# A four-stage network on one core: x loaded in pieces, a shorter FFN prelude, x parked inside the FFN loop, Mamba's constant rows made once

## The chip, the cores and the metric

The kernel runs on one core of a Trainium2 chip. The core has TensorE (PE; its weight loads are listed as PEld), VectorE (DVE), ScalarE (ACT), GpSimd (POOL) and SyncE (SP), which here only issues DMAs and handles semaphores. The metric is the device time of one execution in microseconds (us).

## The reference

The input x has 4,096 rows of 256 values. Four stages follow each other, and each adds a layer norm of its result to x:

```
x = x + LN(attention(LN(x)))     16 heads, causal linear attention, features elu + 1
x = x + LN(ffn(LN(x)))           256 -> 1024 -> 256, exact gelu
x = x + LN(mamba(LN(x)))         two layers, 512 channels, 16 states, a scan over all rows
x = x + LN(moe(LN(x)))           8 experts, the best 2 of each row
```

Three details matter here. The FFN's weights get a low-rank addition made of sixteen of its own input rows (rows 1 to 16 of LN(x)): W1 gets scale times the outer products of four pairs of them, W2 the same of four other pairs. The Mamba layers read LN(x) as their stream and add to it in place, so the x from before must be kept until the end of the stage. And a Mamba layer's velocity v = 0.6 v + input is computed as matrix products with constant powers of 0.6.

## The kernel before

All of x lies in SBUF as `x_res`: 32 tiles of 128 rows, the residual stream of all stages. A chunk is 512 rows, four tiles; there are NCH = 8. Each stage is a phase, `net.run(phase)`. A phase first raises its counting semaphores by one on SP (`start`, L88), then a barrier, then the work of the five engines side by side, each with an instruction order written out by hand, and at its end another barrier and the clearing of all its semaphores on SP (L99). Nothing of a phase starts before this is through.

**Start** (`build`, L2186, L2187): one DMA brings the 4 MB of x, a second the identity, and SP waits for both. Only then attention starts. Its six weight DMAs are issued at L189 to L194, and VectorE, ScalarE and TensorE all wait for them (`loaded`) first. VectorE makes the statistics of chunk 0 (L119, L123), GpSimd the inverse root (L111, L113), VectorE normalises (L234), TensorE transposes (L386), ScalarE copies (L326). Four projections (L395) follow, each into the one bank HEAD: ScalarE makes exp (L330, L334), VectorE the feature (L240), and only then the next projection may start.

**FFN** (`ffn_phase`): five weight DMAs (L518 to L522). Tile 0 is normalised (L552), and sixteen DMAs bring rows 1 to 16 of it from their partitions to partition 0 (L526). TensorE makes the products of the pairs: 8 calls for W1 (L633) and 32 for W2 (L642); each call in f32 is two instructions in the trace. VectorE adds them (L560, L564). Then the loop. TensorE: `hidden(i)` (L661), transposes `head(i+1)` (L652), `result(i)` (L670). VectorE: `head(i+1)` (statistics L119, L123, normalisation L576), `tail(i)` (L583, statistics of z, L590, x + z at L595). GpSimd makes the inverse root for each.

**Streaming in** (`stream_in`, `normalise_all`, a phase of its own): SP stores all of x to DRAM as `parked` in one DMA (L1450). VectorE makes the statistics of all 32 tiles, GpSimd one inverse root, and VectorE, after `parked` has landed, normalises x in place (L1480).

**Mamba** (`mamba_phase`, twice): SP issues 18 loads (L757 to L765), of which the last six are constant rows: three copies of powers of 0.6 in `Mf` and in `Gf`. All engines wait for all 18. VectorE then writes the bf16 high and low parts of these rows into the rows from SUB on of M2, once for each of its 2 * NSUB = 8 places: casts at L989 and L990, subtractions at L997, and the like into Gc (L992, L993, L999). `const_done` counts the two steps. ScalarE waits for the first of them ahead of the floor (L1124), GpSimd and TensorE for the second. GpSimd's first root (L890, L892) and with it the first normalised chunk (L1139), the transposes (L1272), the in-projection (L1284) and all that follows come behind that wait. TensorE first zeroes two banks (L1263). M2 is first read by the velocity products (L1372).

**MoE** (`moe_phases`) reads `parked` back in its first phase.

## Time and profile before

The median of three timed runs is 4020.06 us (4019.51 to 4025.07). The profiled execution took 4023.78 us, of which the trace spans 4022.0.

| stretch, us | what runs | PE busy, us | DVE busy, us | granted PE clock |
|---|---|---|---|---|
| 0 to 17.8 | x loaded | 0 | 0.0 | idle |
| 17.8 to 58.5 | attention's first chunk | 18.5 | 9.7 | 0.92 |
| 58.5 to 446.5 | attention | 370.7 | 226.0 | 0.83 |
| 446.5 to 495.3 | FFN prelude | 22.7 | 11.2 | 0.50 |
| 495.3 to 733.5 | FFN loop | 230.8 | 69.1 | 0.99 |
| 733.5 to 770.3 | streaming in | 0 | 23.2 | idle |
| 770.3 to 858.7 | Mamba 0, prelude | 28.5 | 33.8 | 0.64 |
| 858.7 to 2036.7 | Mamba 0 | 1033.2 | 852.7 | 0.95 |
| 2036.7 to 2125.3 | Mamba 1, prelude | 28.3 | 33.9 | 0.64 |
| 2125.3 to 3258.0 | Mamba 1 | 1017.0 | 852.1 | 0.97 |
| 3258.0 to 4022.0 | MoE | 517.3 | 426.4 | 0.79 |

Over the whole span PE is busy 81%, DVE 63%, ACT 48% and POOL 52%. A stretch's time is what counts for the sum; busy shares tell which engine could set it. The clock is the mean that the throttle granted to TensorE, 1.0 being full speed; where PE is idle it means nothing.

### The profile page before, as it was taken

How to read it: one execution, taken by the hardware profiler on the slowest of the kernel's cores; microseconds unless marked ns; L12 is line 12 of the kernel's file. 1: busy time of each engine (PE TensorE's matmuls, PEld its weight loads, DVE VectorE, ACT ScalarE, POOL GpSimd, SP SyncE). 2: the span in 40 equal slices, each digit the busy share in tenths (PEclk: the TensorE clock that was granted, in tenths of full speed). 3: DMA queues.
4: the chain of work that ended last, by engine and by line, in shares of the span. 5: the costliest groups of instructions: out<-in, count | busy, mean ns of one | idle time of the engine just before them, and what ended most of it. 6: DMA issues, size and time to landing. Idle time of an engine off the chain costs nothing. (4 is left out here: it accounts for less than half of the span.)

```text
span 4022.0 us, 67053 instructions
## 1 busy us (share of the span) xinstructions
PE 3267.0 (81%) x20668; PEld 2263.8 (56%) x20669; DVE 2538.1 (63%) x3759; ACT 1942.4 (48%) x4180; POOL 2075.5 (52%) x1328
## 2 busy tenths in 40 slices
PE   5999699269888988989938999898998843899970
PEld 3777566145555555555515555555555533788860
DVE  2656323547777777777736777777777767554545
ACT  1222022057666666666526766767667633233320
POOL 0000000137677777777725777877778765222216
PEclk8888699689999999999969999999999965899995
DMA  1000000113223222232212232322323234111113
GB/s 55 1 0 0 23 0 0 62 39 84 55 58 80 53 66 71 56 74 63 60 36 63 56 83 55 79 59 62 75 55 83 57 123 138 51 47 47 47 45 110
DMA packets 151616, 228.30 MB, mean 57 GB/s; under 512 B 25250, under 2 KB 84034, under 8 KB 149700
## 3 DMA queue, kind: packets, MB, share of 16 engines
q1 hardware_dynamic: 143300, 202.30, 18.7%
q0 software_dynamic: 8064, 23.08, 2.0%
q8 instruction: 105, 1.72, 0.2%
q14 instruction: 147, 1.20, 0.1%
HBM read 119.99 MB, written 23.59 MB: 36 GB/s over the span
## 5 line engine op out<-in xcount | busy, mean ns | idle before, releaser
L943 POOL TENSOR_TENSOR m_hc<-m_h,m_Cb 128x1024 f32<-128x1024 f32 x512 | 1234.5, 2415 | 413.0 <-PE m_bank L1354 255.3
L1080 DVE TENSOR_TENSOR_SCAN m_h<-m_dA,m_vel 128x1024 f32<-128x1024 f32 x512 | 1169.1, 2283 | 93.0 <-ACT m_dA L1220 50.0
L1354 PE MATMUL m_bank<-m_hc,ident 128*128 128x512 f32 x2048 | 1055.1, 630 | 102.4 <-POOL m_hc L943 102.1
L1220 ACT ACTIVATE m_dA<-m_delta,m_rate 128x255 f32<-128x255 f32 x2048 | 874.1, 497 | 46.2 <-DVE m_h L1080 26.0
L1370 PE MATMUL m_vel<-m_M,m_U 128*128 128x128 bf16 x4096 | 542.9, 222 | 76.1 <-DVE m_h L1080 58.3
L1354 PEld LDWEIGHTS m_bank<-m_hc,ident 128*128 128x128 f32 x2048 | 362.1, 197 | 323.2 <-issue 222.5
L1372 PE MATMUL m_vel<-m_M,m_U 112*128 112x128 bf16 x4096 | 542.7, 222 | 0.0
L1370 PEld LDWEIGHTS m_vel<-m_M,m_U 128*128 128x128 bf16 x4096 | 403.0, 99 | 211.1 <-DVE m_h L1080 102.2
L1372 PEld LDWEIGHTS m_vel<-m_M,m_U 112*128 112x128 bf16 x4096 | 407.0, 99 | 82.1 <-issue 70.3
L1284 PE MATMUL m_bank<-m_pair,m_in 128*128 128x256 f32 x1024 | 280.1, 401 | 68.8 <-DVE m_cv L1020 63.1
L1069 DVE TENSOR_TENSOR m_vel<-m_vel,m_entry 128x4 f32<-128x4 f32 x512 | 82.5, 161 | 366.8 <-PE m_vel L1372 363.8
L1284 PEld LDWEIGHTS m_bank<-m_pair,m_in 128*128 128x128 f32 x1024 | 194.8, 198 | 189.2 <-DVE m_cv L1020 100.1
L2037 ACT ACTIVATE x_h<-x_bank,x_b 128x256 f32<-128x256 f32 x320 | 134.4, 471 | 283.9 <-PE x_bank L1983 267.7
L1943 POOL DMA_INDIRECT x_x_in<-xn_rows,r_from_row x80 | 91.1, 1138 | 347.9 <-PE x_bank L1967 299.7
L1983 PE MATMUL x_bank<-x_xhi,r_wlo 128*128 128x256 bf16 x640 | 175.5, 274 | 5.7 <-issue 5.0
L111 POOL TENSOR_SCALAR var_eps<-a_zmv 128x1 f32<-128x1 f32 x32 | 7.1, 223 | 328.0 <-DVE a_zmv L299 328.0
L1983 PE MATMUL x_bank<-x_xlo,r_whi 128*128 128x256 bf16 x640 | 175.2, 274 | 0.0
L1983 PE MATMUL x_bank<-x_xhi,r_whi 128*128 128x256 bf16 x640 | 175.2, 274 | 0.0
L1996 PE MATMUL x_bank<-r_whi,x_hlo 128*128 x640 | 174.5, 273 | 0.0
L1996 PE MATMUL x_bank<-r_whi,x_hhi 128*128 x640 | 174.4, 273 | 0.0
L1996 PE MATMUL x_bank<-r_wlo,x_hhi 128*128 x640 | 174.4, 273 | 0.0
L933 POOL TENSOR_TENSOR m_u<-m_u,m_zs 128x1024 f32<-128x1024 f32 x34 | 80.0, 2352 | 172.2 <-DVE m_u L1055 172.2
(281 smaller groups left out, 5570.5 us busy)
## 6 DMA issues: line engine op xcount, KB each, us to landing
m_Cb<-m_c_rows SPq DMA_DIRECT2D x256, 256.0 KB, 3.2
m_M<-m_Mhi SPq DMA_DIRECT2D x128, 256.0 KB, 4.3
m_M<-m_Mlo SPq DMA_DIRECT2D x64, 256.0 KB, 3.9
m_U<-m_Uhi SPq DMA_DIRECT2D x128, 128.0 KB, 3.2
y_rows<-x_y SPq DMA_DIRECT2D x40, 256.0 KB, 2.1
m_U<-m_Ulo SPq DMA_DIRECT2D x64, 128.0 KB, 3.3
g_stage<-in_e_w SPq DMA_DIRECT2D x8, 1024.0 KB, 5.5
o_stage<-in_e_w SPq DMA_DIRECT2D x16, 512.0 KB, 4.2
```

The source lines that it names most:

```text
L943: nc.gpsimd.tensor_tensor(hc[:, g].rearrange("p m a t -> p m (a t)"), h[:, p % 2, 2 * g:2 * g + 2].rearrange("p m a t -> p m (a t)"), Cb[: ...
L1069: nc.vector.tensor_tensor(heads, heads, entry[:, p, 2 * g:2 * g + 2, :], ALU.add).then_inc(s["fix_done"], 1)
L1080: nc.vector.tensor_tensor_scan(flat(h), flat(dA), VB[:, 2 * g * 512:2 * (g + 1) * 512], 0.0, ALU.mult, ALU.add).then_inc(s["scan_done"], 1)
L1220: nc.scalar.activation(dA[:, p % 2, m, a, 1:CM], delta[:, par, m, 1:CM], ACT.Exp, scale=rate[:, m, NG * p + a:NG * p + a + 1]).then_inc(s[ ...
L1284: last = nc.tensor.matmul((H0, H1)[g % 2][:, m % 2 * CM:(m % 2 + 1) * CM], w_in[:, k, m * P:(m + 1) * P], xT[:, k, :], start=(k == 0), sto ...
L1354: last = nc.tensor.matmul(Y[g][:], net.ident[:], hc[:, g, :, a, :], start=(p == 0 and a == 0), stop=(p == NPAIR - 1 and a == NG - 1))
L1370: nc.tensor.matmul(to, U1[:, par, j, m * P:(m + 1) * P], M1[:, par, j, NG * p:NG * p + NG, :], start=True, stop=False)
L1372: last = nc.tensor.matmul(to, U2[:, par, j, m * P:(m + 1) * P], M2[:, par, j, NG * p:NG * p + NG, :], start=False, stop=True)
L1943: nc.gpsimd.indirect_dma_start(x_in[:, par, t, :], None, xn_rows, bass.IndirectOffsetOnAxis(from_row[:, at:at + 1], 0)).then_inc(s[f"x_in{ ...
L1983: last = nc.tensor.matmul(out, w_part[:, bass.ts(e * WB + kk * KH + m, P)], x_part[:, par, kk, :], start=(kk == 0 and n == 0), stop=(kk == ...
L1996: last = nc.tensor.matmul(YB[par][:, t * D:(t + 1) * D], h_part[:, par, m, t * P:(t + 1) * P], w_part[:, bass.ts(e * (WB // 2) + KD * KH / ...
L2037: last = nc.scalar.activation(h[:, g % 2, m % 2, :], HB[g][:, m % 2 * SLOT:(m % 2 + 1) * SLOT], ACT.Relu, bias=b1[:, bass.ts(e[par] * KH + ...
```

## The change

1. x is loaded by chunks. SP issues chunk 0 and the identity and waits for neither. The other seven follow in attention's block, behind its six weight DMAs. Each has a semaphore `x_in[c]`, for which VectorE waits ahead of a chunk's first statistics; TensorE waits for the identity. Behind them SP issues the FFN's five weight DMAs, into tiles that now live through both phases.
2. In attention's opening, ScalarE, TensorE and VectorE wait for the weights later. The four first projections go to the four banks S[g] without a wait between them, and the statistics of chunk 1 stand between the third and the fourth feature.
3. The FFN's sixteen token DMAs become two: a store of the sixteen rows to DRAM and, after a wait, a load of all onto partition 0. The products for W2 are 8 calls of 256 columns for 32 of 64, in another order of columns.
4. `stream_in` is gone. In the FFN's `tail(i)` VectorE also makes the statistics of the new x, SP stores each chunk to `parked` when its sum is done, GpSimd makes a third root per chunk, and `stream(i)` normalises the chunk in place once both are through. In the loop `stream(i-1)` stands ahead of `head(i+1)`.
5. In Mamba the six constant loads come first, with a semaphore of their own. VectorE makes the high and low rows for place 0 alone, and seven DMAs copy them to the other places of M2. TensorE waits for these ahead of the first velocity. ScalarE's wait for `const_done` is gone.

The core of the diff (semaphore declarations are left out):

```diff
 # build and attention
-                sp.dma_start(net.x, dram["x"].rearrange("(n p) d -> p n d", p=P)).then_inc(stored, 16)
-                sp.dma_start(net.ident[:], dram["ident"]).then_inc(stored, 16)
-                sp.wait_ge(stored, 32)
+                sp.dma_start(net.x[:, 0:TPC, :], net.x_rows[:, 0:TPC, :]).then_inc(net.x_in[0], 16)
+                sp.dma_start(net.ident[:], dram["ident"]).then_inc(net.ident_in, 16)
...
+                for c in range(1, NCH):
+                    tiles = slice(c * TPC, (c + 1) * TPC)
+                    sp.dma_start(net.x[:, tiles, :], net.x_rows[:, tiles, :]).then_inc(net.x_in[c], 16)
+                net.ffn.load(sp, dram)
...
                 for g in range(4):
-                    feature(0, 0, g)
+                    dve.wait_ge(qk_exp, 1 + g + 1)
+                    nc.vector.scalar_tensor_tensor(phi[:, 0, g, :], S[g][:], 0.0, exps[:, g % 2, :],
+                                                   ALU.max, ALU.add).then_inc(phi_done, 1)
+                    if g == 2:
+                        stats(1)
+                masks(0, 0)
                 normal(1)
-                masks(0, 0)
...
+                pe.wait_ge(loaded, LOADS)
+                pe.wait_ge(xT_done, 1 + KD)
                 for g in range(4):
-                    project(0, 0, g)
+                    for k in range(KD):
+                        last = nc.tensor.matmul(S[g][:], wqkv[:, k, g * P:(g + 1) * P], xT[:, 0, k, :],
+                                                start=(k == 0), stop=(k == KD - 1))
+                    last.then_inc(qk_psum, 1)
 # FFN
-                for r in range(4 * RANK1):
-                    sp.dma_start(tok[:, r, :], xn[1 + r:2 + r, 0, :]).then_inc(tok_done, 16)
+                sp.dma_start(tok_rows, xn[1:1 + 4 * RANK1, 0, :]).then_inc(tok_kept, 16)
+                sp.wait_ge(tok_kept, 16)
+                sp.dma_start(tok[0:1].rearrange("p r d -> p (r d)"), tok_rows.rearrange("r d -> (r d)").unsqueeze(0)).then_inc(tok_done, 16)
+
+                for c in range(NCH):
+                    sp.wait_ge(x_done, 1 + c + 1)
+                    if c >= 1:
+                        sp.wait_ge(parked, 16 * c)
+                    tiles = slice(c * TPC, (c + 1) * TPC)
+                    sp.dma_start(net.parked[:, tiles, :], x[:, tiles, :]).then_inc(parked, 16)
+                sp.wait_ge(parked, 16 * NCH)
...
-                for m in range(KH):
-                    r, half = m // 2, m % 2
-                    for i in range(RANK1):
-                        col = (m % 2) * D + i * (D // 4)
-                        last = nc.tensor.matmul(B[4 + m // 2][:, col:col + D // 4],
-                                                tok[0:1, 2 * (RANK1 + i) + 1, half * P:(half + 1) * P],
-                                                tok[0:1, 2 * (RANK1 + i), r:D:4], start=True, stop=True)
+                for i in range(RANK1):
+                    for half in range(2):
+                        to = B[4 + i][:].rearrange("p (r a o) -> p a r o", a=2, o=D // 4)[:, half]
+                        of = tok[0:1, 2 * (RANK1 + i), :].rearrange("p (o r) -> p r o", r=4)
+                        last = nc.tensor.matmul(to, tok[0:1, 2 * (RANK1 + i) + 1, half * P:(half + 1) * P], of,
+                                                start=True, stop=True)
...
+                def stream(i):
+                    dve.wait_ge(n_rstd, 1 + i + 1)
+                    dve.wait_ge(parked, 16 * (i + 1))
+                    for j in range(TPC):
+                        last = nc.vector.tensor_scalar(x[:, i * TPC + j, :], x[:, i * TPC + j, :], mv2[:, j, 0:1],
+                                                       rstd2[:, j:j + 1], ALU.subtract, ALU.mult)
+                    last.then_inc(n_done, 1)
+                    dve.wait_ge(n_done, 1 + i + 1)
+                    dve.sem_inc(net.carrier, 1)
 
                 head(0)
-                with dve.Fori(0, NCH - 1) as i:
+                head(1)
+                tail(0)
+                with dve.Fori(1, NCH - 1) as i:
+                    stream(i - 1)
                     head(i + 1)
                     tail(i)
+                stream(NCH - 2)
                 tail(NCH - 1)
+                stream(NCH - 1)
 # Mamba
+                for part in range(3):
+                    at = SUB + part * NS
+                    sp.dma_start(Mf[at:at + NS, 0], dram["decay"][SUB:SUB + NS]).then_inc(s["const_in"], 16)
+                    sp.dma_start(Gf[at:at + NS, 0], dram["carry_on"]).then_inc(s["const_in"], 16)
...
+                sp.wait_ge(s["const_done"], 1 + 2)
+                for at in range(1, 2 * NSUB):
+                    sp.dma_start(M2[SUB:KV, at // NSUB, at % NSUB], M2[SUB:KV, 0, 0]).then_inc(s["const_moved"], 16)
...
-                    for j in range(NSUB):
-                        nc.vector.tensor_copy(M2[SUB:SUB + 2 * NS, par, j], Mf[SUB:SUB + 2 * NS, 0])
-                        nc.vector.tensor_copy(M2[SUB + 2 * NS:KV, par, j], Mf[SUB + 2 * NS:KV, 0])
+                dve.wait_ge(s["const_in"], CONSTS)
+                for rows in (slice(SUB, SUB + 2 * NS), slice(SUB + 2 * NS, KV)):
+                    nc.vector.tensor_copy(M2[rows, 0, 0], Mf[rows, 0])
+                    last = nc.vector.tensor_copy(Gc[rows], on[rows])
+                last.then_inc(s["const_done"], 1)
                 dve.wait_ge(s["const_done"], 1 + 1)
-                for par in range(2):
-                    for j in range(NSUB):
-                        nc.vector.tensor_tensor(M2[SUB + 2 * NS:KV, par, j], Mf[SUB + 2 * NS:KV, 0],
-                                                M2[SUB + 2 * NS:KV, par, j], ALU.subtract)
+                nc.vector.tensor_tensor(M2[SUB + 2 * NS:KV, 0, 0], Mf[SUB + 2 * NS:KV, 0],
+                                        M2[SUB + 2 * NS:KV, 0, 0], ALU.subtract)
...
-                act.wait_ge(s["const_done"], 1 + 1)
...
+                        pe.wait_ge(s["const_moved"], COPIES)
```

## Rows read from the trace of the kernel before

**Rows 1.** Windows: stretch, its us, busy us (instructions) by engine, PEclk, DMA share, GB/s.

```profile
58.50:446.50 388.00, 370.70 (x2339) 292.76 (x2338) 226.03 (x580) 86.33 (x180) 33.57 (x76) 0.83 0.00 1
```

**Rows 2.** Timeline of the start: start us, us, engine, line, what, [idle before <-releaser].

```profile
0.74 0.45 SPq L2186 DMA_DIRECT2D x_res<-in_x  x1
17.80 0.33 SPq L189 DMA_DIRECT2D wqkv<-in_wqkv  x1
18.28 0.51 DVE L222 MEMSET a_vt<- 128x544 f32 x1
23.88 1.40 DVE L119 BATCH_NORM_STATS2 a_st<-x_res 128x6 f32<-128x256 f32 x4 [5.09 <-DMA parity<-in_parity]
33.87 3.78 PE L395 MATMUL a_bank<-a_xT,wqkv 128*128 128x512 f32 x4 [0.67 <-ACT a_xT L326]
38.97 0.69 DVE L240 SCALAR_TENSOR_TENSOR a_phi<-a_bank,a_exps 128x512 f32<-128x512 f32 x1 [8.40 <-ACT a_exps L334]
56.12 2.07 PE L405 MATMUL a_bank<-wqkv,a_xT 128*128 128x256 f32 x4 [2.07 <-DVE a_phi L240]
```

**Rows 3.** Timeline of the FFN prelude.

```profile
452.57 0.41 DVE L552 TENSOR_SCALAR f_xn<-x_res,f_mv,f_rstd 128x256 f32<-128x256 f32 x1 [1.18 <-POOL f_rstd L113]
464.59 7.19 PE L633 MATMUL f_bank<-f_tok 1*128 1x256 f32 x16 [21.45 <-DMA f_tok<-f_xn]
471.58 13.75 PE L642 MATMUL f_bank<-f_tok 1*128 1x64 f32 x64
495.28 4.93 PE L661 MATMUL f_bank<-f_xT,f_w 128*128 128x512 f32 x6 [1.30 <-ACT f_xT L611]
```

**Rows 4.** Timeline of one turn of the FFN loop.

```profile
669.46 13.90 PE L661 MATMUL f_bank<-f_xT,f_w 128*128 128x512 f32 x32
676.98 1.41 DVE L119 BATCH_NORM_STATS2 f_st<-x_res 128x6 f32 x4 [0.62 <-DVE x_res L595]
680.45 1.38 DVE L576 TENSOR_SCALAR f_xn<-x_res,f_mv,f_rstd 128x256 f32 x4 [1.66 <-POOL f_rstd L113]
683.19 1.04 PE L652 MATMUL f_bank<-ident,f_xn 128*128 128x128 f32 x8
698.12 13.90 PE L661 MATMUL f_bank<-f_xT,f_w 128*128 128x512 f32 x32
```

**Rows 5.** Timeline at the ends of the FFN and of Mamba's first layer.

```profile
732.27 1.23 DVE L595 TENSOR_TENSOR x_res<-x_res,f_zn 128x1024 f32<-128x1024 f32 x1
770.32 0.34 SPq L757 DMA_DIRECT2D m_norm<-in_m_norm  x1
2027.33 0.69 DVE L1061 TENSOR_TENSOR x_res<-x_res,m_bank 128x512 f32<-128x512 f32 x1 [7.96 <-PE m_bank L1343]
2036.75 0.34 SPq L757 DMA_DIRECT2D m_norm<-in_m_norm  x1
```

**Rows 6.** Timeline of Mamba's first prelude.

```profile
780.79 0.26 ACT L1118 ACTIVATE m_rate<-m_rate 128x64 f32<-128x64 f32 x1 [9.18 <-DMA m_Gf<-in_carry_on]
793.59 0.20 ACT L1124 ACTIVATE m_floor<-m_floor 128x1 f32<-128x1 f32 x1 [12.26 <-DVE m_Gc L993]
795.76 0.40 ACT L1133 ACTIVATE m_pair<-x_res 128x256 f32<-128x256 f32 x1
803.19 0.19 POOL L890 TENSOR_SCALAR m_mean<-m_ssq 128x2 f32<-128x2 f32 x1 [29.07 <-DVE m_Gc L999]
806.53 0.70 PE L1272 MATMUL m_bank<-ident,m_pair 128*128 128x128 f32 x4
814.73 1.99 PE L1284 MATMUL m_bank<-m_pair,m_in 128*128 128x256 f32 x8 [2.85 <-DVE m_cv L1020]
```

**Rows 7.** DMA issues: out<-in, queue, count, KB of each, median us from issue to landing.

```profile
x_res<-in_x SPq DMA_DIRECT2D x1, 4096.0 KB, 13.9
g_residual<-parked SPq DMA_DIRECT2D x8, 512.0 KB, 4.6
out_x<-x_res SPq DMA_DIRECT2D x8, 512.0 KB, 3.1
m_c_rows<-m_small SPq DMA_DIRECT2D x32, 16.0 KB, 1.4
```

More of the change, by code:

```diff
@@ L65, in __init__ @@
         self.own_pool = ctx.enter_context(nc.semaphore("own_pool"))
+        self.x_rows = dram["x"].rearrange("(n p) d -> p n d", p=P)
+        self.x_in = [ctx.enter_context(nc.semaphore(f"x_in{c}")) for c in range(NCH)]
+        self.ident_in = ctx.enter_context(nc.semaphore("ident_in"))
     def sb(self, ctx, name, shape, dt=F32):
@@ L103, in _, with __init__, load @@
                         sp.sem_clear(used)
+class FfnWeights:
+    LOADS = 5 * 16
+    def __init__(self, net, ctx):
+        self.w1 = net.sb(ctx, "f_w1", [P, KD, HID])
+        self.w2 = net.sb(ctx, "f_w2", [P, KH, D])
+        self.b1 = net.sb(ctx, "f_b1", [P, KH])
+        self.b2 = net.sb(ctx, "f_b2", [P, D])
+        self.scale = net.sb(ctx, "f_scale", [P, 1])
+        self.loaded = ctx.enter_context(net.nc.semaphore("f_loaded"))
+    def load(self, sp, dram):
+        sp.dma_start(self.w1[:], dram["f_w1"]).then_inc(self.loaded, 16)
+        sp.dma_start(self.w2[:], dram["f_w2"]).then_inc(self.loaded, 16)
+        sp.dma_start(self.b1[:], dram["f_b1"]).then_inc(self.loaded, 16)
+        sp.dma_start(self.b2[:], dram["f_b2"].partition_broadcast(P)).then_inc(self.loaded, 16)
+        sp.dma_start(self.scale[:], dram["f_scale"].partition_broadcast(P)).then_inc(self.loaded, 16)
 def inverse_root(net, pool, out, variance):
@@ L2185, in _ @@
             def _(sp):
-                sp.dma_start(net.x, dram["x"].rearrange("(n p) d -> p n d", p=P)).then_inc(stored, 16)
-                sp.dma_start(net.ident[:], dram["ident"]).then_inc(stored, 16)
-                sp.wait_ge(stored, 32)
+                sp.dma_start(net.x[:, 0:TPC, :], net.x_rows[:, 0:TPC, :]).then_inc(net.x_in[0], 16)
+                sp.dma_start(net.ident[:], dram["ident"]).then_inc(net.ident_in, 16)
+        with ExitStack() as weights:
+            net.ffn = FfnWeights(net, weights)
+            net.run(attention_phase)
+            net.run(ffn_phase)
         for phase in phases:
-            if phase in (mamba_phases, moe_phases):
-                phase(net)
-            else:
-                net.run(phase)
+            phase(net)
 def layout(a):
```

143 lines of the change are left out of this document (51 added, 92 removed).

## The prediction, made before the changed kernel ran

> **What bounds the kernel now.** I read the busy times per stage first, in the table of windows. The two Mamba layers take 2,355 us, and inside their loops the work is shared by four engines; the change leaves these loops as they are. The places it touches are the seams between the stages, so the question at each seam is which wait ends last. I then read the timeline at each seam, and the DMA issues for transfer times.
>
> Five stretches matter. Until 17.8 us no engine computes: everything waits for x, one DMA. Then x's statistics wait 5.1 us more, until 23.88, for the last of six small loads that they don't use [rows 2]. After it the first four projections share one PSUM bank, so matmul, ScalarE and VectorE alternate until 56.12 [rows 2]. Attention's own loop then has PE nearly always busy, yet the mean granted clock is 0.83 [rows 1]. In the FFN prelude PE idles 21.45 us for sixteen small DMAs and then runs 80 instructions at the lower clock [rows 3]. The FFN loop is bound by PE: hidden, transposes and result follow each other without a gap, 28.66 us a chunk (669.46 to 698.12 [rows 4]). Between 733.5 and 770.3 PE is idle. In each Mamba prelude the constant rows, made eight times over on VectorE, release GpSimd, TensorE and ScalarE [rows 6].
>
> **The change, part by part.** All sums are made against the profiled execution, 4023.78 us by its own time (span 4022.0), which is 3.7 above the median 4020.06.
>
> *1. x in pieces.* SP now issues x's first 512 KB at 0.74 and the identity, waits for nothing, and is through at about 1.7. Starting a phase costs semaphore operations. Between the two Mamba layers 130 of them (66 cleared, 64 raised) take from 2028.02 to 2036.75, 8.73 us, or 0.067 each [rows 5]; attention raises 32, 2.1 us, so its block starts near 3.9. Two memsets take until 1.0 us after that [rows 2]. A 512 KB transfer lands 3.1 to 4.6 us after its issue [rows 7], so at 3.8 to 5.3. I take the statistics at 5.1, against 23.88: **-18.8**. The weights, first in the queue of the new block, land some 6.1 us after its start as before (23.88 - 17.80), at 10.0. They are needed by the first projection, 10.0 us after the statistics (33.87 - 23.88), at 15.1, so they are covered. The other seven pieces and the FFN's 2.1 MB are queued behind them; 4 MB took 13.9 us [rows 7], so all lie in SBUF long before VectorE reaches them.
>
> *2. Four banks for the first projections.* Before: 33.87 to 56.12, 22.25 us, in four rounds of about 5.8 (3.78 matmul, about 1.3 on ScalarE, 0.69 on VectorE [rows 2]). Now 16 matmul instructions of 512 columns run back to back. At the lower level one takes 0.86, at the higher 0.43 (32 in 13.90 [rows 4]). When the FFN starts the same way, 6 take 4.93 [rows 3] and all later ones are fast. So the groups end at about 3.8, 5.9, 7.6 and 9.3. Behind the last: ScalarE 1.3. But VectorE now makes the second chunk's statistics (1.8) between the third and the fourth feature: it starts them at 9.6, ends at 11.4, and the fourth feature ends at 12.2. Gain 22.25 - 12.2 = **-10**; with the clock low to the end, the last group ends at 14.0 and the gain is 6.2; without the interposed statistics it would be 11.
>
> *3. FFN prelude.* Weights come early: no gain by itself, as they had landed before the first product. Token rows: their source is ready at 452.98, and the first product waits until 464.59 [rows 3]. Now one 16 KB store and, after its wait, one 16 KB load. A 16 KB store lands in 1.4 [rows 7]. The load I bound between 1.4 and 4.6 and take at 2.0, nearer to the small one. The product starts near 456.6: -8.0. The second product has 16 instructions of 256 columns for 64 of 64. Such a one took 7.19/16 = 0.45, so 7.2 for 13.75: -6.6. Five more semaphores raised: +0.3. Together **-14.3**; with the load at 4.6 it would be -11.7.
>
> *4. The parking and the streaming in the FFN loop.* This adds a wait. In each loop turn VectorE now goes: stream(i-1), head(i+1), tail(i). stream(i-1) waits for GpSimd's root and for the parking DMA of the sum just made; head(i+1) is queued behind it, and PE's transposes wait for head(i+1). Let T be the start of hidden(i), 669.46 in the turn I read [rows 4]. x's sum is done at T+6.9 (676.98 less 0.62). From the start of statistics to the start of the normalisation that uses them takes 3.47 (676.98 to 680.45). So the streaming statistics, begun at T+7.1, allow the normalisation at T+10.6; the parking DMA lands at T+10.1 to T+11.6 (3.1 to 4.6). The normalisation takes 1.38, so head(i+1) starts at T+12.1 instead of T+7.5, and its own normalisation at T+15.6 instead of T+11.0. PE's transposes start at T+13.7 now and end at T+14.8 [rows 4]. In the changed kernel they wait for the first tile until about T+16.1 and for the fourth until T+17.0, and end at T+17.3. PE stalls 2.5 us a turn. head(0) and head(1) come ahead of tail(0), so six turns pay: **+15**. If the parking lands at 4.6, each pays 1 more: +21. What would hide this is slack of VectorE ahead of the transposes; there are 2.7 us of it (T+13.7 less T+11.0), and about 4.7 are added.
>
> *5. The tail and the dropped pass.* Before, the last sum ends at 733.50 [rows 5] and Mamba starts at 770.32: 36.8. Now the last chunk's statistics and root allow its normalisation after 0.2 + 3.5, the parking after 3.2 to 4.7; with 1.4 for it the block ends about 5.3 later. 27 semaphores are then cleared and 64 raised, 91 times 0.067 = 6.1, and some 0.3 of barriers. Mamba starts 11.8 after the sum: **-25**, or -24 with the later landing.
>
> *6. Mamba's constant rows.* VectorE's 24 large operations (16 casts, 8 subtractions) become 3, and 7 DMAs copy the result to the other places. The constants are loaded first, so VectorE ends before the 18 loads have landed, which they do 10.5 us after the block's start (780.79 - 770.32) [rows 6]. ScalarE's floor was released only at 793.59; now at 781.3, after the two small rate operations. From there to the end of the squares takes 2.6 (796.16 - 793.59). GpSimd takes them up near 784.2, against 803.19, where it was released by the constants. PE's zeroing products (3.75 us) moved ahead of the gap, no longer in the way. So **-19** for each of the two layers, -38. The largest load is issued 2.8 us later, which may cost up to 1.5 a layer; and the zeroing products no longer lead straight into the transposes, so that the next 16 products may run at the lower level, up to 3.7 more. Seven more issues on SP sit ahead of its first store, over 20 us before that is wanted; the copies themselves are first needed by the velocity products, over 60 us after the start. Both cost nothing; without that cover, about 4 us a layer.
>
> Sum: -18.8 - 10 - 14.3 + 15 - 25 - 38 = -91. From 4023.8 that gives 3932.7; from the median, 3929. I say 3930.
>
> **A rule that speaks against it.** In the preludes PE resumed after 2.85 us without work at full pace, 8 products of 256 columns in 1.99 [rows 6], the higher level (2.4 GHz). So my sum has the stall of 2.5 us in part 4 without a price in clock. The Trainium skill (TensorE: Matmul & The Clock Gate, "HAM oscillation — how this bites in real kernels") warns that idle waits between groups of matmuls let the clock fall again, each group then starting cold. By the row that rule costs nothing here; by the rule, taken for every stall, the time is the first rival's.
>
> **The rivals.**
> - *The clock falls at each stall.* For it: attention has a mean clock of 0.83 though PE is busy 370.7 of 388 us [rows 1]. Against: the 2.85 us gap. The FFN's first hidden ran 4.3 us at the lower level (495.28 to 499.6) [rows 3], which costs 2.15. Six times: +13, 3943. Chance 14%.
> - *No stall in the loop.* VectorE would have to find 2.5 us. Nothing in the rows gives them. 3930 - 15 = 3915. Chance 10%.
> - *The weights share the DMA engines with x's other pieces and the FFN's weights*, and land after 6.8 MB instead of first; at 4 MB in 13.9 us that is 24 us after 3.9. The first projection waits until 27.9 instead of 15.1: +13, 3943; +5 if only x's pieces interfere. Against it: one queue, weights first. 9%.
> - *Slower.* In the FFN loop the stall keeps PE at the lower level (1.2 GHz) for good. A chunk takes 57.3 instead of 28.66; eight chunks cost 229: 4159. It decides from 91/28.7 = 3.2 such chunks on. For it: attention's loop spends about a third of its time low. Against: its matmuls are short, and the FFN's, even with the stall, keep PE busy nine tenths of the time. 2%.
>
> **Numbers.** The forecast holds 65%. A measurement of this kernel tells about 0.2%, 8 us. Range 3910 to 3952: below, no stall and a short landing; above, the clock rival with a late parking. Only the last rival lies above 4020: faster 0.97, same 0.01, slower 0.02.
>
> **What would show it.** VectorE's first statistics near 5 us; the fourth first feature 12 us after the first projection; the first token product about 4 us after its row; in the FFN loop a PE gap of 2 to 3 us ahead of six of the transposes, released by VectorE, and turns of 31.2 us; Mamba's start 12 us after the last sum; GpSimd's first root 14 us after each Mamba start. A gain under 70 or over 115 would mean that a loop I called unchanged has moved.

## The result, and the profile after

Changed kernel: 3916.81 us, median of 4 runs (3912.37 to 3922.45); before, on the same chip, 4019.78 (4015.5 to 4025.07). Ratio 0.9744, 95% interval 0.9727 to 0.9761: faster by 103 us. The profiled execution took 3916.93, its span is 3915.0 (before 4022.0), so 107.0 us have to be found. The table has the landmarks of the two traces.

| landmark | before | after | difference so far | this step | forecast |
|---|---|---|---|---|---|
| first statistics | 23.88 | 5.13 | -18.75 | -18.75 | -18.8 |
| first projection | 33.87 | 13.77 | -20.10 | -1.35 | 0 |
| first tile's values | 56.12 | 25.66 | -30.46 | -10.36 | -10 |
| last sum of attention ends | 446.48 | 411.72 | -34.76 | -4.3 | 0 |
| first hidden product of the FFN | 495.28 | 446.78 | -48.50 | -13.7 | -14.3 |
| last sum of the FFN ends | 733.50 | 708.06 | -25.44 | **+23.1** | +15 |
| Mamba's first layer starts | 770.32 | 719.78 | -50.54 | -25.1 | -25 |
| GpSimd's first root there | 803.19 | 735.52 | -67.67 | -17.1 | -19 |
| Mamba's second layer starts | 2036.75 | 1927.32 | -109.43 | **-41.8** | 0 |
| GpSimd's first root there | 2070.04 | 1943.15 | -126.89 | -17.5 | -19 |
| MoE starts | 3259.04 | 3151.72 | -107.32 | **+19.6** | 0 |

The seams are where they were forecast. The two largest departures lie inside Mamba's loops, whose code is the same in both kernels.

The start after, answering [rows 2] (timeline: start us, us, engine, line, what, [idle before <-releaser]):

```profile
4.22 1.28 ACT L359 ACT_TABLE_LOAD   x1 [4.06 <-PEq L91]
5.13 1.34 DVE L142 BATCH_NORM_STATS2 a_st<-x_res 128x6 f32<-128x256 f32 x4
13.77 9.23 PE L514 MATMUL a_bank<-a_xT,wqkv 128*128 128x512 f32 x16 [0.77 <-ACT a_xT L359]
24.95 0.66 DVE L337 SCALAR_TENSOR_TENSOR a_phi<-a_bank,a_exps 128x512 f32<-128x512 f32 x1
25.66 1.13 PE L439 MATMUL a_bank<-wqkv,a_xT 128*128 128x256 f32 x4 [2.66 <-DVE a_phi L337]
```

The statistics no longer wait for a DMA: they stand right behind the memset. The 16 projections are one run of 9.23 us (forecast 9.3), and the fourth feature starts 11.2 after it began. The 1.35 us I had not counted: ScalarE's table load (1.28 us) now lies at 4.22, ahead of the data; before, it stood at 30.14, behind the first transposes and ahead of the copy which the first projection needs.

The FFN's prelude, answering [rows 3] (same columns):

```profile
418.19 0.41 DVE L605 TENSOR_SCALAR f_xn<-x_res,f_mv,f_rstd 128x256 f32<-128x256 f32 x1 [1.18 <-POOL f_rstd L136]
418.63 0.34 SPq L562 DMA_DIRECT2D tok_rows<-f_xn  x1
420.07 0.27 SPq L564 DMA_DIRECT2D f_tok<-tok_rows  x1
422.40 7.19 PE L710 MATMUL f_bank<-f_tok 1*128 1x256 f32 x16 [14.00 <-DMA f_tok<-tok_rows]
429.39 7.43 PE L719 MATMUL f_bank<-f_tok 1*128 1x256 f32 x16
446.78 2.07 PE L737 MATMUL f_bank<-f_xT,f_w 128*128 128x512 f32 x2 [1.31 <-ACT f_xT L688]
```

Store and load together take 3.8 us from the finished row to the first product, 0.2 more than forecast.

One turn of the FFN loop, answering [rows 4]:

```profile
641.05 13.90 PE L737 MATMUL f_bank<-f_xT,f_w 128*128 128x512 f32 x32
648.11 1.40 DVE L652 BATCH_NORM_STATS2 f_st<-x_res 128x6 f32 x4 [0.16 <-DVE x_res L648]
651.95 1.38 DVE L664 TENSOR_SCALAR x_res<-x_res,f_mv,f_rstd  x4 [1.91 <-POOL f_rstd L136]
653.68 1.41 DVE L142 BATCH_NORM_STATS2 f_st<-x_res 128x6 f32 x4 [0.35 <-DVE x_res L664]
657.16 1.38 DVE L629 TENSOR_SCALAR f_xn<-x_res,f_mv,f_rstd 128x256 f32 x4 [1.65 <-POOL f_rstd L136]
657.62 1.41 PE L728 MATMUL f_bank<-ident,f_xn 128*128 128x128 f32 x8 [2.68 <-DVE f_xn L629]
672.69 1.88 PE L737 MATMUL f_bank<-f_xT,f_w 128*128 128x512 f32 x4
```

The chain has the forecast order: the streaming statistics at T+7.1, the normalisation of x at T+10.9 (T = 641.05), released by GpSimd's root and not by the parking, then the next chunk's statistics at T+12.6, and PE waits 2.68 us for VectorE ahead of its transposes. The turn is 31.64. Of the six turns with a stall three are like this one and three are 33.2 to 33.3. Windows of one of each:

```profile
576.07:607.72 31.65, 28.97 (x105) 18.94 (x104) 12.42 (x41) 7.75 (x11) 3.79 (x6) 1.00 0.05 17
607.72:641.05 33.33, 30.66 (x106) 20.13 (x105) 12.41 (x41) 7.74 (x11) 3.79 (x6) 0.95 0.05 16
```

(Stretch, its us, busy us (instructions) of PE, PEld, DVE, ACT and POOL, PEclk, DMA share, GB/s.) In the longer turn the granted clock is at the lower level for 3.4 us, from 1.4 us after PE has resumed. (The first turn, 31.12, has no stall; PE starts it at the lower clock, as before.)

The seam to Mamba and Mamba's first prelude, answering [rows 5, 6]:

```profile
706.83 1.23 DVE L648 TENSOR_TENSOR x_res<-x_res,f_zn 128x1024 f32<-128x1024 f32 x1
719.78 0.34 SPq L834 DMA_DIRECT2D m_Mf<-in_decay  x1
731.90 0.26 ACT L1196 ACTIVATE m_rate<-m_rate 128x64 f32<-128x64 f32 x1 [10.83 <-DMA m_decay<-in_decay]
731.92 3.42 PE L1340 MATMUL m_bank<-m_hc,ident 128*128 128x512 f32 x4 [30.48 <-DMA m_decay<-in_decay]
735.52 0.19 POOL L970 TENSOR_SCALAR m_mean<-m_ssq 128x2 f32<-128x2 f32 x1 [11.95 <-ACT m_pair L1210]
739.17 6.63 PE L1361 MATMUL m_bank<-m_pair,m_in 128*128 128x256 f32 x16 [0.93 <-ACT m_pair L1221]
```

ScalarE and PE are now released by the loads, no longer by the constants. They land 12.1 us after the block's start, not 10.5: that is the 1.5 us a layer which the forecast allowed and did not count. The 16 products that follow run in part at the lower clock, 6.63 us for 3.72 before, as the forecast also allowed; it costs nothing here, since from GpSimd's first root to the first addition to x it is 85.4 us after and 85.2 before.

Mamba's loops. I measure a turn from one addition to x (L1139) to the next; windows: stretch, its us, busy us (instructions) of PE, PEld, DVE, ACT and POOL, PEclk, DMA share, GB/s. After, second layer, a short turn and a long one:

```profile
2313.95:2384.47 70.52, 65.11 (x408) 40.97 (x407) 54.00 (x58) 48.86 (x108) 54.31 (x30) 0.95 0.27 67
2384.47:2460.53 76.06, 66.97 (x408) 42.60 (x407) 54.32 (x58) 49.11 (x108) 54.31 (x30) 0.93 0.25 63
```

Same instructions, nearly the same busy time on VectorE, ScalarE and GpSimd, 1.9 us more on TensorE, and 5.6 us more in all. I call a turn long when it takes over 73 us. Every second turn is such a long one, but only in some layers: six in the first layer before and none in the second, none and five after. From first to last addition the two loops take 1138.9 + 1098.0 = 2236.9 us before and 1096.9 + 1117.0 = 2213.9 after. So the loops give -23.0 and all the rest -84.0.

### The profile page after: what moved, and what is told of

The parts are those of the page before. It is cut to its first block and busy times, and to the rows that moved or that the text cites. A ratio compares the mean times of both kernels' runs of the same rounds, so it can differ in the third digit from the quotient of the medians.

```text
span 3915.0 us, 67006 instructions
## 1 busy us (share of the span) xinstructions
PE 3257.2 (83%) x20620; PEld 2255.4 (58%) x20621; DVE 2504.7 (64%) x3717; ACT 1942.4 (50%) x4180; POOL 2077.8 (53%) x1340
## 5 line engine op out<-in xcount | busy, mean ns | idle before, releaser
L1448 PE MATMUL m_vel<-m_M,m_U 128*128 128x128 bf16 x4096 | 542.8, 222 | 89.0 <-DVE m_h L1158 65.1
L1448 PEld LDWEIGHTS m_vel<-m_M,m_U 128*128 128x128 bf16 x4096 | 402.8, 99 | 222.6 <-DVE m_h L1158 110.3
```

The costliest lines, as they stand in the source:

```text
L1448: nc.tensor.matmul(to, U1[:, par, j, m * P:(m + 1) * P], M1[:, par, j, NG * p:NG * p + NG, :], start=True, stop=False)
```

## The experiments

"Loops" is the sum of the two Mamba loops as just defined, from each run's profile; "rest" is the span less that. Each ratio is to the kernel before as timed on the same chip as the run (medians 4016.67 to 4022.40).

| kernel | median us | ratio to before, 95% interval | span | loops (turns over 73 us by layer) | rest |
|---|---|---|---|---|---|
| before | 4019.78 | | 4022.0 | 2236.9 (6, 0) | 1785.1 |
| changed | 3916.81 | 0.9744 (0.9727-0.9761) | 3915.0 | 2213.9 (0, 5) | 1701.1 |
| e1 head first | 3898.40 | 0.9697 (0.9675-0.972) | 3898.6 | 2216.0 (0, 5) | 1682.6 |
| e2 old constants | 3982.00 | 0.9912 (0.989-0.9934) | 3979.4 | 2244.9 (4, 6) | 1734.5 |
| e3 pass apart | 3940.42 | 0.9799 (0.978-0.9819) | 3943.5 | 2237.7 (4, 5) | 1705.8 |
| e4 shift | 3926.62 | 0.9767 (0.9746-0.9788) | 3925.0 | 2214.4 (0, 5) | 1710.6 |
| e5 changed again | 3916.68 | 0.9743 (0.9726-0.9759) | 3917.5 | 2211.7 (0, 5) | 1705.8 |
| e6 body of four | 3888.10 | 0.9674 (0.9657-0.969) | 3885.8 | 2205.7 (2, 2) | 1680.1 |
| e7 old token rows | 3900.35 | 0.9706 (0.969-0.9722) | 3897.6 | 2211.5 (0, 4) | 1686.1 |
| e8 one bank | 3908.77 | 0.9727 (0.9711-0.9743) | 3903.3 | 2211.7 (0, 3) | 1691.6 |
| e9 before, straight | 3970.27 | 0.9884 (0.9854-0.9914) | 3972.3 | 2190.3 (0, 0) | 1782.0 |
| e10 changed, straight | 3885.14 | 0.9673 (0.9652-0.9693) | 3883.7 | 2179.5 (0, 0) | 1704.2 |
| e11 head first, straight | 3862.10 | 0.9614 (0.9597-0.9632) | 3856.1 | 2181.0 (0, 0) | 1675.1 |
| e12 late weights | 3900.15 | 0.9706 (0.9688-0.9724) | 3897.9 | 2215.9 (0, 5) | 1682.0 |

**e1: the next head ahead of the stream.** Tests the stall of part 4.

```diff
 with dve.Fori(1, NCH - 1) as i:
-    stream(i - 1)
     head(i + 1)
+    stream(i - 1)
     tail(i)
```

> The changed kernel with one edit: in VectorE's FFN loop the next chunk's head stands ahead of stream(i-1), as before the change. Theory (the stall is a matter of queue order): the head's normalisation is back near T+13 from the start of a turn, PE's transposes wait for nothing, turns are 28.7 us instead of the 31.7 and 33.3 measured, the FFN's part (first hidden to last sum) falls from 261.3 to about 239, and the time from 3916.8 to about 3895. Rival (the third statistics and root simply overload VectorE and GpSimd in the loop): turns stay above 31 us and the time within 5 us of 3917.

One turn in e1 (timeline):

```profile
538.15 13.90 PE L737 MATMUL f_bank<-f_xT,f_w 128*128 128x512 f32 x32
547.54 1.41 DVE L142 BATCH_NORM_STATS2 f_st<-x_res 128x6 f32 x4 [0.41 <-issue]
551.01 1.38 DVE L629 TENSOR_SCALAR f_xn<-x_res,f_mv,f_rstd 128x256 f32 x4 [1.65 <-POOL f_rstd L136]
551.88 1.04 PE L728 MATMUL f_bank<-ident,f_xn 128*128 128x128 f32 x8
566.81 3.60 PE L737 MATMUL f_bank<-f_xT,f_w 128*128 128x512 f32 x8
```

The head comes at T+9.4 in place of T+12.6, the transposes wait for nothing, and the turn is 28.66 again. From the first hidden product to the last sum's end it is 238.8 us, against 261.3: 22.5 of the table's +23.1 were VectorE's order.

**e2: Mamba's constants as before**, all else changed. That part of the change taken back: VectorE makes the constants eight times over, and the others wait for them.

```diff
-for rows in (slice(SUB, SUB + 2 * NS), slice(SUB + 2 * NS, KV)):
-    nc.vector.tensor_copy(M2[rows, 0, 0], Mf[rows, 0])
+for par in range(2):
+    for j in range(NSUB):
+        nc.vector.tensor_copy(M2[SUB:SUB + 2 * NS, par, j], Mf[SUB:SUB + 2 * NS, 0])
+        nc.vector.tensor_copy(M2[SUB + 2 * NS:KV, par, j], Mf[SUB + 2 * NS:KV, 0])
...
```

> The changed kernel with Mamba's constant rows as before the change (loads last, 16 casts and 8 subtractions on VectorE, ScalarE's wait back). Theory (the preludes gave 17 us each and Mamba's loops are untouched): 3916.8 + 34 = 3951. Rival (the 23 us by which the two Mamba loops together became shorter in the trace come from where their turns fall against TensorE's clock, which every edit ahead of them shifts): the two loops' lengths change again, by 7 us for each turn with a second stretch at the lower clock, and the time lies anywhere between 3925 and 3990; the trace shows how many turns of over 74 us there are.

The rest grows by 33.4, the part's real worth (preludes -17.1 and -17.5 in the table). The loops grow by 31.0, with ten long turns for five (and three more of 72.4 to 72.9). A reading of the total alone would have called the constants worth 65 us.

**e3: the parking and normalisation as a pass of their own**, between FFN and Mamba, as before.

```diff
 with dve.Fori(1, NCH - 1) as i:
-    stream(i - 1)
     head(i + 1)
     tail(i)
...
+net.run(lambda n: stream_in(n, net.parked))
```

> The changed kernel with the parking and normalising of x as before, in a pass of its own after the FFN (its FFN loop is that of before too; some unused semaphores are still cleared, 0.4 us). Theory: the FFN's turns are back at 28.66 us, which gives back 23 us, and Mamba starts 37 us after the last sum instead of 11.7, which costs 25: 3916.8 + 2 = 3919, apart from what Mamba's loops do. Rival (the fused pass is worth its 25 us in full): 3942.

The rest grows by 4.7 only: the pass costs 25.5 more between the stages (Mamba starts 37.2 after the last sum, in the changed kernel 11.7), and the FFN loop, at 28.66 a turn again, gives 23.3 back (238.0 us for 261.3). As it was written, streaming into the FFN's tail was worth next to nothing. The other 24 us by which the span grows are the loops; by the total alone, 3940, the rival's 3942 would have been right.

**e4: a shift of 50 semaphore operations on SP ahead of Mamba**, nothing else.

> The changed kernel with 50 more semaphore operations on SP between the FFN and Mamba, nothing else: a shift of 3.3 us. If Mamba's loops don't depend on when they start: 3916.8 + 3.3 = 3920. If the number of turns with a second low stretch of the clock depends on it, the two loops (1126.4 and 1146.5 in the trace) change by several us, up to 20 either way.

The loops don't move (2214.4); the rest grows by 9.5, of which the 50 operations are 3.2 and attention 4.4. Mamba starts 7.5 us later in all, and the same turns are long.

**e5: the changed kernel once more.**

> The changed kernel once more, unchanged, on another profile. The question is Mamba's loops: in the profile of the changed kernel the first layer's loop had no long turn and the second's five (73 to 79 us in place of 70.5), in that of the kernel before six and none. Theory A: which turns are long belongs to the program (the address of its code, the order of its waits), and this run shows 0 and 5 again, loops of 1097 and 1117 us, 3915 to 3920 us as a whole. Theory B: it is drawn anew in each execution: another pattern than 0 and 5, and the time scatters with it, by up to 40 us for two layers with long turns against two without. If A holds, differences of the loops between kernels are repeatable but still no part of the edit.

The same pattern, (0, 5), and loops within 2.2 us. The long turns belong to the program. What does change between two executions of one program is attention: from the first tile's values to the start of its last sum 385.6 us in the first profile and 390.2 here; before took 389.9, and all fourteen profiles lie between 383.4 and 390.2. The -4.3 in the table can't be told from this scatter.

**e6: four chunks to a loop body.**

```diff
-with pe.Fori(1, NCM // 2 - 1) as c2:
-    slots(c2 * 2, 0, True, True)
-    slots(c2 * 2 + 1, 1, True, True)
+with pe.Fori(0, NCM // 4 - 1) as c4:
+    for n in range(4):
+        slots(c4 * 4 + 2 + n, n % 2, True, True)
```

(on all engines; VectorE and SP have their first two chunks ahead of the loop.)

> The changed kernel with the next turn's head ahead of the last one's stream in the FFN (as e1), and in Mamba the loop body written out for four chunks in place of two, so that each layer goes round its loop 3 times in place of 6 or 7 on every engine. The long turns of the Mamba loops were always every second one, those that hold the way back to the loop's start. Theory A: the way back costs it (fetching code again, engine by engine, until TensorE waits long enough for its clock to fall): then at most 2 to 3 turns of a layer are long, the loops together take 2194 + at most 20 us, against 2216 in e1, and the time falls by 5 to 15 us to 3883 to 3893. Rival B: the long turns follow the buffers' parity or the engines' order at even chunks: they stay at every second turn, 5 or more in a layer, and the time stays at 3898 or goes over it. Rival C: the longer code costs something of its own and all turns grow: over 3905.

Windows of e6, second layer:

```profile
2295.28:2365.35 70.07, 64.40 (x408) 40.17 (x407) 53.98 (x59) 48.85 (x108) 54.27 (x30) 0.98 0.27 68
2365.35:2439.80 74.45, 65.70 (x408) 42.15 (x407) 54.15 (x59) 49.07 (x108) 54.35 (x30) 0.95 0.25 65
```

In each layer two turns are long (over 73 us), from chunk 5 to 6 and from 9 to 10, exactly the two at which a body of four goes back; with bodies of two they were 3 to 4, 5 to 6, and so on to 11 to 12, and in some layers also 1 to 2, where only VectorE and SP, whose loops start with the first chunk, go back. They follow the way back, and not the parity of the buffers.

What happens there, in the changed kernel, around 2435 us (PE, then ScalarE):

```profile
2435.42 0.29 PE L1448 MATMUL m_vel<-m_M,m_U 128*128 128x128 bf16 x1 [2.84 <-issue]
2436.47 3.73 PE L1431 MATMUL m_bank<-m_hc,ident 128*128 128x512 f32 x4
2433.95 1.70 ACT L1297 ACTIVATE m_dA<-m_delta,m_rate 128x255 f32<-128x255 f32 x4 [1.84 <-issue]
```

The 16 small matmuls at the top of PE's body stop after six for 2.84 us, and "issue" says that the engine waited for nothing which the profile shows. ScalarE stops likewise. Then the clock is down: four products on m_hc take 3.73 us, where shortly after, at 2442.54, the same four take 1.93. So this long turn is a stop of TensorE of about 3 us plus what the clock costs after it.

That is not the account of all of them. ScalarE's stop is in every layer with a loop of two chunks, 1.6 to 2.6 us at each of its five ways back, also where no turn is long: the first line below is from the changed kernel's first layer. In the first layers of e2 and e3 it is VectorE that stops, for 3.2 to 3.6 us at each of its six ways back (second line, e2), and TensorE at most 1.0. In before's first layer, which has the longest turns, neither has such a stop by name (TensorE at most 0.8); there VectorE's scan waits 6.23 us, ended by ScalarE, and TensorE's in-projection 5.36 for VectorE (last two lines, before). Which stop is behind that wait the profile doesn't tell.

```profile
1222.28 1.70 ACT L1297 ACTIVATE m_dA<-m_delta,m_rate 128x255 f32<-128x255 f32 x4 [2.19 <-issue]
1244.08 2.29 DVE L1156 TENSOR_TENSOR_SCAN m_h<-m_dA,m_vel 128x1024 f32<-128x1024 f32 x1 [3.27 <-issue]
1304.21 2.29 DVE L1080 TENSOR_TENSOR_SCAN m_h<-m_dA,m_vel 128x1024 f32<-128x1024 f32 x1 [6.23 <-ACT m_dA L1220]
1309.14 2.07 PE L1284 MATMUL m_bank<-m_pair,m_in 128*128 128x256 f32 x4 [5.36 <-DVE m_cv L1020]
```

In e6's four long turns too it is VectorE that stops (3.3 to 3.6), and TensorE at most 0.9. And not every stop makes a turn long: in e7 and e8, of ten stops of TensorE of 2.4 us and more, three lie in turns of 71.3 to 72.3.

**e7: the token rows by 16 DMAs** (on e1).

```diff
-sp.dma_start(tok_rows, xn[1:1 + 4 * RANK1, 0, :]).then_inc(tok_kept, 16)
-sp.wait_ge(tok_kept, 16)
-sp.dma_start(tok[0:1]..., tok_rows...).then_inc(tok_done, 16)
+for r in range(4 * RANK1):
+    sp.dma_start(tok[:, r, :], xn[1 + r:2 + r, 0, :]).then_inc(tok_done, 16)
```

> As e1 (next turn's head first in the FFN), with the 16 token rows again fetched by 16 separate DMAs of one row each on SP, in place of one DMA to memory and one back; the FFN's weights still come early. My theory: of the 14.1 us that the FFN's prelude lost, the DMAs carry about 9 (the kernel before issued the last row some 12.9 us after the normalised row, the changed one has all 16 after 3.8) and the weights' early loading the rest; so the first hidden matmul comes 8 to 10 us later than in e1 (449.4), and the time is about 3907. Rival: the weights' wait was what ended last, and the rows cost nothing: 3898.

```profile
418.02 10.10 SPq L563 DMA_DIRECT2D f_tok<-f_xn  x16
429.32 7.19 PE L709 MATMUL f_bank<-f_tok 1*128 1x256 f32 x16 [21.53 <-DMA f_tok<-f_xn]
```

SP needs 10.10 us to issue them. From the start of attention's last sum to the first hidden product it is 42.99 us, in e1 35.38: the two DMAs are worth 7.6 (forecast 8.0). The median moves by only 2: attention was 3.2 us and the loops 4.5 us shorter in this profile.

**e8: the first projections through one bank** (on e1).

```diff
-for g in range(4):
-    for k in range(KD):
-        last = nc.tensor.matmul(S[g][:], ...)
-    last.then_inc(qk_psum, 1)
+for g in range(4):
+    project(0, 0, g)
```

> As e1 (next turn's head first in the FFN), with the first chunk's four projections again through one bank, so that each waits for the feature map of the one before it, as in the kernel before; x in pieces and all else kept. My theory: the values of the first tile start 10 us later (35.7 in place of 25.7 us from the start), all of it on the chain, and the time is about 3908. Rival: part of the 10 us is taken back in the attention loop, whose TensorE clock then comes up with other idle stretches before it: the last attention sum starts less than 5 us later than in e1 (413.99), 3898 to 3903.

The values start at 35.72, 10.1 later than in e1, and the last attention sum 8.6 later. Attention scatters by up to 4.6 us between two executions (e5), so the 8.6 alone could be more or less; but the median moves by 10.4 as well. The gain of part 2 reaches the end nearly whole, and the rival's 3898 to 3903 doesn't hold.

**e12: the FFN's weights late** (on e1): `net.ffn.load(sp, dram)` in the FFN's block.

> As e1 (next turn's head first in the FFN), with the FFN's weights loaded only at the FFN's start, ahead of the token rows on the same queue, as the kernel before did; the rows still go by two DMAs. Of the 14.1 us which the prelude lost, e7 put 7.6 on the rows (last attention sum to first hidden matmul 42.99 in e7, 35.38 in e1). Theory: the weights are the rest, since they stand ahead of the rows on SP and share the DMA engines with them: 4 to 7 us from the last attention sum to the first hidden matmul, and the time about 3904. Rival: the weights come while the stall on the rows lasts anyway, and the rest is clock: under 2 us, 3898 to 3900.

```profile
417.55 0.48 SPq L562 DMA_DIRECT2D tok_rows<-f_xn  x1
423.87 0.27 SPq L564 DMA_DIRECT2D f_tok<-tok_rows  x1
426.17 7.19 PE L710 MATMUL f_bank<-f_tok 1*128 1x256 f32 x16 [19.08 <-DMA f_tok<-tok_rows]
```

The store's wait ends 6.3 us after its issue, behind 2.1 MB of weights, where it took 1.4 in the changed kernel; from attention's last sum to the first hidden product 40.56, +5.2. Time: 3900, as attention was 3.7 shorter here. The two edits depend on each other: by SP's 16 issues, 10.10 us long, the weights are hidden, and beside one short store they are not. Of the table's -13.7 the products for W2 are 6.3 (7.43 us for 13.75). From the last sum to the first hidden product e7, with the old rows, early weights and new products, takes 42.99, and before less these 6.3 takes 42.9: early weights alone give nothing. e12, with new rows and late weights, takes 40.56: new rows alone give 2.4. Both together give 7.5.

**e9, e10, e11: no loop at all.** All 16 chunks of Mamba written out, in the kernel before, in the changed one, and in e1:

```diff
-with pe.Fori(1, NCM // 2 - 1) as c2:
-    slots(c2 * 2, 0, True, True)
-    slots(c2 * 2 + 1, 1, True, True)
+for c in range(2, NCM - 2):
+    slots(c, c % 2, True, True)
```

> The kernel before with Mamba's 16 chunks written out one after the other on every engine, no loop at all; the rest as before. In its profile the two loops took 2236.9 us (six long turns in the first layer), without long turns they would take about 2194. Theory A, that the way back to the loop's start is what makes a turn long: no long turn, the loops 2190 to 2200, the time about 3980. Rival B: straight code costs as much where it must be fetched: long turns stay or all turns grow, 4020 or more.

> The changed kernel, likewise with no loop in Mamba. Theory A: its loops fall from 2213.9 to about 2194, the time from 3917 to about 3897; against e9, with the loops' long turns out of both, the change is then worth what stands outside the loops, 84 us (my sum said 91). Rival B: 3917 or more; or the distance to e9 is the 103 us of the two medians, and then the loops had no part in it.

> The changed kernel with the next turn's head first in the FFN (as e1) and with no loop in Mamba: all that has been found in one kernel. Theory A: 3898.4 less the 22 us of long turns in e1's loops, 3876 to 3880, 8 to 12 below e6 with its four chunks to a body. Rival: the three turns back of e6 cost about what the longer code costs, and it ends at e6's 3888 or above.

One turn of e11's second layer (windows), and then the idle time of PE ahead of the velocity matmuls over seven turns, in e11 (L1444) and in the changed kernel (L1448; 2097 to 2605 us):

```profile
2136.66:2206.52 69.86, 62.79 (x408) 39.78 (x407) 54.10 (x59) 48.87 (x108) 54.27 (x30) 1.00 0.27 68
```

```profile
L1444 PE MATMUL m_vel<-m_M,m_U x896: 216/219/314, 2067.6 to 2553.4; 128*128 128x128 bf16 x180
its engine sat idle before it (us, times) until:
  DVE m_h L1156: 16.7, 7
  issue: 0.9, 2
```

```profile
L1448 PE MATMUL m_vel<-m_M,m_U x896: 219/219/314, 2099.2 to 2602.3; 128*128 128x128 bf16 x180
its engine sat idle before it (us, times) until:
  DVE m_h L1158: 15.5, 8
  issue: 9.1, 5
```

No turn is over 71.7 us, on no layer of the three kernels, and the unexplained stops of TensorE here fall from 9.1 to 0.9 us. The loops take 2190.3, 2179.5 and 2181.0. In e10 and e11 that is below the 2194 which I took as the floor, so both came in lower than expected (3885 for 3897, 3862 for 3876 to 3880): the short turns of a loop, at 70.5, cost more than the 70.0 of straight code. Straight code isn't all alike either: in e9's second layer five turns in a row take 71.7, and its loops are 10.8 longer than e10's. These five are the turns in which GpSimd's unexplained stops add up to most, 4.0 us; whether they are the cause no run shows. e11 is the best version: 3862.10 us, ratio 0.9614 (0.9597 to 0.9632), against 0.9744 for the change as given. And e9 against e10, both without a way back, leaves the change itself: spans -88.6, medians -85.1; outside the loops -77.8, where the looped pair gave -84.0. Of the 6.2 us between these two 4.3 are attention's scatter (e9's was 1.9 shorter than before's, e10's 2.4 longer than the changed kernel's).

**The queues that fetch code.** The DMA view of each profile also counts the packets of two instruction queues, q8 and q14 (queue, kind: packets, MB, share of 16 engines). In the changed kernel's second layer, the long turn from 2384.47 and then the short one that follows:

```profile
q8 instruction: 6, 0.10, 0.6%
q14 instruction: 3, 0.02, 0.1%
```

```profile
q8 instruction: 3, 0.05, 0.3%
q14 instruction: 2, 0.02, 0.1%
```

Counted over a layer's whole loop, this sorts all layers of the profiles with bodies of two chunks, and those with no loop. The last three columns have the longest idle time with "issue" as its cause in each turn with a way back (in straight code: in any of the first fourteen turns), us:

| packets of q8, q14 in the loop | layers | long turns | loop, us | TensorE | VectorE | ScalarE |
|---|---|---|---|---|---|---|
| 17, 40 to 45 | before 2; first layer of changed, e1, e4, e5, e7, e8, e12 | none | 1094 to 1098 | 0 to 0.3 | 0 | 1.6 to 2.3 |
| 63, 40 | second layer of changed, e1, e3, e4, e5, e7, e8, e12 | 3 to 5 | 1114 to 1122 | 2.4 to 3.1 | 0 | 1.6 to 2.1 |
| 17, 75 | first layer of e2 and e3 | 4 | 1116 to 1121 | 0 (once 1.0) | 3.2 to 3.6 | 1.7 to 2.3 |
| 63, 70 | e2's second | 6 | 1124 | 2.8 to 3.1 | 0 | 1.6 to 2.4 |
| 62, 75 | before 1 | 6 | 1139 | 0.2 to 0.8 | 0 | 1.7 to 2.6 |
| 49 or 50, 45 or 46 (no loop) | e9, e10, e11, both | none | 1089 to 1100 | 0 to 1.3 | 0 to 0.2 | 0 to 0.2 |

(VectorE's six ways back are 1 to 2, 3 to 4 and so on; the other two engines' five begin with 3 to 4.)

In the changed kernel's first layer q8 moves nothing at all once the loop has gone round; q14 moves 5 packets in a turn with a way back and 1 in the turns between, and that makes no turn long. In its second layer each turn with a way back has 6 packets of q8 and the turns between have 3; in the first layer of before it is 5 and 9 (q8, q14) against 4 and 2, and the turns are longest. e6's four long turns, too, have the most packets of their layers (5 of q8 with 7 or 11 of q14). Wherever q8 has 63 packets TensorE stops (in before's first layer, with 62, it does not), and where q14 has 75 beside q8's 17 VectorE does. Straight code fetches 95 packets a layer, hardly fewer than the 103 of the changed kernel's second layer, but spread over the turns (q8 at 3 or 4 a turn), and TensorE, VectorE and ScalarE have no stop over 1.3 us in a layer's first fourteen turns (in the last but one TensorE stops for up to 3.0 in e10 and e11). (GpSimd has more there than in a loop, 2.1 to 4.0 us in all but two of the turns for some 0.5, and no turn is over 71.7.) So what costs is not how much is fetched, but a larger fetch after a jump. The Trainium skill says as much (Runtime: NRT & Kernel Launch, "Instruction fetch mechanics"): code is fetched ahead in order only, and a taken branch to a place that is not in the engine's window has to wait for a DMA. The trace agrees, with 2.84 us on PE shortly after such a branch in the changed kernel's second layer; in its first, PE takes the same branch and doesn't stop.

## Why the prediction held, and where it didn't

- *Part 1, start (-18.8).* Right, 18.75; the table load gave 1.35 besides.
- *Part 2, four banks (-10).* Right, 10.36; e8 puts 8.6 on the end of attention, within its scatter, and 10.4 on the median.
- *Part 3, FFN prelude (-14.3).* Right in sum (13.7 in the table, with the block's start), and the store and load at 3.8 against 3.6. The products gave 6.3 of the 6.6. "Weights come early: no gain by itself" is true only beside the 16 old DMAs: beside the new ones it is 5.2 (e12), and the rows' 8.0 (7.6) hangs on it.
- *Part 4, the stall (+15).* The order of the waits is right in every link, the price of the clock was not; the size was +23.1, outside the +21 allowed for a late parking, which did not occur. The stall is 2.5 to 2.7 on PE, and the turn 3.0 longer rather than 2.5, since the transposes themselves run against VectorE (1.41 for 1.04). The other 5 us are clock: three of the six turns have a stretch of 3.4 us at the lower level and are 1.6 to 1.7 longer. I had weighed this with a gap of 2.85 us after which PE went on at full pace [rows 6] and priced it at nothing. A gap of 2.67 or 2.68 us costs nothing in one turn and 1.7 us in the next: one row at the higher level is no bound. The Trainium skill's rule (TensorE: Matmul & The Clock Gate, "HAM oscillation — how this bites in real kernels") was right in direction, and the trace agrees for half of the stalls: in the other three the clock doesn't fall, and where it does it falls 1.4 to 1.6 us after PE has resumed. The rival built on it, +13 for six, was too high.
- *Part 5, the dropped pass (-25).* Right, 25.1. But parts 4 and 5 are one edit, and together they are -2, as e3 shows with 4.7 on the rest. With e1's order 22.5 of the 23.1 come back, and the edit is worth about what I had listed as its gain.
- *Part 6, constants (-38).* 34.6 (e2: 33.4). The mis-sized term is the loads: 12.1 us in place of 10.5, as six constants go first.
- *"The change leaves these loops as they are."* This failed, and outside every rival. The code of the loops is the same in both kernels. The term was put at nothing without a row for it; the loops moved by -42 and +19, net -23, which is why the profiled time is 3917 and not the 3933 that the sum gave; outside the loops it is -84 against -91. That the number came so near is in part luck: had the loops stood still it would have been 3940, still in the range, and the measured 3917 lies close to the range's lower end, which was set for a loop with no stall, while the stall was there and larger than forecast. My sign of it, "a gain under 70 or over 115", stayed silent at 103: two moves of opposite sign had nearly met. Only the landmarks showed them. e5 shows that the pattern belongs to the program, e6 that the long turns are at the way back, e9 to e11 that they go with the loop, and the instruction queues that they are turns with more code fetched. What is argued, and not shown: that it is the place of a body in memory that decides whether it stays in an engine's buffer, which engine each of the two queues serves (q8's packets go with TensorE's stops and q14's with VectorE's, no more), and what stops in the first layer of before, where the -42 comes from. No run moved the code alone. The loops of e9 and e10, with no way back in either, still differ by 10.8 us.

## What to carry to other kernels

Ahead of reading an edit's worth from a total, split off the loops whose code it doesn't touch: here the two together moved by up to 31 us for edits outside them (e2), and the one program that was profiled twice showed the same pattern again, so that more runs don't average it out; the packets of the instruction queues tell them apart. When work is put into a loop's slack, put it behind whatever the bounding engine waits for next: the same instructions cost 23 us in one order and less than 1 in the other. And a body with few, long turns can be worth writing out: 36 us of 3898 here (e11 against e1), for the same work.

## What the runs showed of the hardware that I had not expected

- At a loop's way back TensorE stopped for 2.84 us in the middle of a group of matmuls and ScalarE for 1.84, with "issue" as the cause, and the lower clock followed. In the same code, a layer before, TensorE has no such stop: ahead of the velocity matmuls of the changed kernel's first layer only VectorE and a DMA are named (14.5 and 1.0 us between 962 and 1455). ScalarE stops there as well, 2.0 to 2.2 us at each way back, and no turn is long.
- An idle gap of nearly the same length (2.55 to 2.68 us) was followed by full pace in one turn and by 3.4 us at the lower level in the next, in alternation; the clock fell only 1.4 to 1.6 us after TensorE had resumed.
- Two executions of one program differ by 4.6 us in attention (385.6 and 390.2), with a mean granted clock of 0.85 and 0.84 there; outside it the spans differ by 2.1 us.
- A small store issued behind 2.1 MB on the same queue came back after 6.3 us, in place of 1.4.
